# The layer normalisation's scaling pass one exponential earlier, and each reciprocal right behind its transposition

## The chip, the cores and the metric

One Trainium2 chip, of which one NeuronCore runs the whole program. The metric is the device time of one launch in microseconds (us). Engine names follow the profile: PE is the matrix engine (PEld its weight loads), DVE the vector engine, ACT the scalar engine, POOL the GpSimd engine, and SP the queue that issues the DMAs.

## The reference

For `x` of shape (8, 512, 1024) and a context of shape (8, 512, 256), float32:

```
xn   = layernorm(x)
q    = xn in 32 heads of 32 columns; k = v = context in 8 heads of 32 columns (4 query heads share one)
w    = softmax(q k^T / sqrt(32))          # 512 x 512 for each batch and query head
x    = x + (w v)                          # cross attention
yn   = layernorm(x)
gate = sigmoid(slope_n * (sum_s (select_n . (yn - mu_n) / |yn - mu_n|)^2 - center_n)),  n = 0..7
n*   = argmax_n gate;  s = max_n gate     # for each row
mod  = bias[n*] + degen[n*] (update[n*]^T (yn - debias[n*]))
out  = x + (1 - s) * yn + s * mod
```

## The kernel before

The attention runs over 64 **units** (8 batches times 8 key heads). A unit is one key head with its 4 query heads: 4 x 4 = 16 **quarters**, where quarter `n` is the 128 keys of block `n // 4` against the 512 queries of head `n % 4`. Each quarter goes through PE (`score_keys`, L596: four matmuls into one PSUM bank), then ACT (L870: the exponential from the bank into `probs`, in SBUF). Three banks take turns for everything that passes here: quarters, the turned tiles of `x`, the turned maxima, and the denominators. A table worked out in Python (`bank_of`, `bank_before`) says which use follows which in a bank, and PE waits for the use before it to be read out.

Each unit is walked in four steps `t` = 0..3, and each engine has its own instruction list, written out in the order of the code and never reordered. In step `t` of unit `u`:

- PE scores, for a unit ahead, the raw maxima (`score_rows`, L558), which DVE reduces (`largest`, L933, 2.29 us each). This is a ping-pong on a single buffer: L558 waits for the last L933, and L933 for L558.
- PE scores a few quarters (L596), multiplies the exponentials with the values (`gather`, L610), and scores the rest of the step's quarters. In an **even** unit the steps take quarters 0-3, 4-8, 9-11 and 12-15; quarters 12 and 13 come ahead of the gather in step 3, and 14 and 15 behind it.
- The denominators of a unit are the column sums of `probs`. POOL adds two key blocks at a time (`front`, L367, and `back`, L357, 4.56 us each), PE multiplies the two sums with ones (L623, L633), DVE transposes the result (`take_denominators`, L945) and takes 16 reciprocals for each partition (`invert`, L951), and POOL multiplies the turned rows with them (`normalise`, L329) and adds them to `x` (L334).

Units go in pairs. Below, E is an even unit and O = E + 1 the odd one behind it. In the pair, one new tile of `x` (128 rows) is prepared for a later batch: DVE takes its statistics (L961, L965, L971, L977), POOL the inverse root (L270, L273), ACT scales and shifts it (`normalise_tile`, L808, 1.23 us) in E, and in O PE turns it in three parts (L584), which ACT and DVE split into two halves of float16 (L819 and L985, L823 and L991). Tiles come to an end before the units do: E = 0, 2, ..., 50 have an L808 among their exponentials, E = 52 to 62 have none.

Behind the 64 units comes the gate stage over 8 batches (L707 to L741, L881, L1071 to L1145), which the change does not touch.

The places the change touches: `NORM_AT` (L198) is the quarter ahead of whose exponential `normalise_tile` stands in ACT's list; `invert` stands in DVE's list in the loop over `u` and `t` (L1047, L1059). Ahead of each exponential ACT waits for the quarter's scores. Ahead of quarters 0, 4, 8 and 12 it also waits for the gather and the POOL sum that last read that part of `probs`; these waits stand in the code ahead of `normalise_tile` for quarter 12.

Of the kernel before, what the change touches and what calls it, by code (L numbers as in the profile page):

```python
# [4 lines left out]
def xattn_ffn(nc: bass.Bass, x, ctx_in, sel_w, sel_mu, imp_center, imp_slope, lora_up, lora_dn,  # L5
# [34 lines left out]
    def wait(eng, sem, count):  # L40

        if not isinstance(count, int) or count > 0:
            eng.wait_ge(sem, count)

    with ExitStack() as keep:
# [55 lines left out]
        with ExitStack() as own:  # L101
# [86 lines left out]
            live = lambda u: 0 <= u < UNITS  # L188
# [6 lines left out]

            BEGIN = ((0, 4, 9, 12, NSC), (0, 5, 10, 13, NSC))
            MIDST = ((2, 6, 11, 14), (2, 7, 12, 15))
            NORM_AT = 13  # L198
            DOWN_AT, FOLD_AT = ((-AHEAD, ST - 1), (1 - AHEAD, 0)), (1 - AHEAD, ST - 1)

            QUARTERS_KEPT = {"score": 0.4, "max": 0.4, "part": 0.95}
# [581 lines left out]
            def _(act):  # L783
# [14 lines left out]
                def make_shift(u):  # L798

                    wait(act, max_turned, u + 1)  # L800
                    wait(act, shift_in[u % 2], 16 * (u // 2))
                    act.activation(shift[:, u % 2, :], st_ps[0:G * ST, bank_of["max", u, 0], 0:P], ACT.Copy,
                                   scale=-1.0 / SHIFT_UNIT).then_inc(shift_made, 1)

                def normalise_tile(n):

                    act.wait_ge(rstd_done, 2 * n + 2)
                    act.activation(x_tile(n), x_tile(n), ACT.Identity, scale=rstd[:, n % 2:n % 2 + 1],  # L808
                                   bias=neg_mean[:, n % 2:n % 2 + 1]).then_inc(xn_done, 1)
# [37 lines left out]
                for u in range(-AHEAD, UNITS):  # L847
                    tile = tile_of(u)
                    for t in range(ST):
# [8 lines left out]
                        if live(u):  # L858
                            s = u % 2
                            for n in range(BEGIN[u % 2][t], BEGIN[u % 2][t + 1]):  # L860
# [4 lines left out]
                                if n == MIDST[u % 2][2] and live(u + 1):  # L865
                                    make_shift(u + 1)
                                if n == NORM_AT and u % 2 == 0 and whole(tile):
                                    normalise_tile(tile)
# [50 lines left out]
            def _(dve):  # L919
                def first_largest(u, t):  # L920

                    for half in range(2):
                        wait(dve, max_scored if half else half_scored, ST * u + t + 1)
                        dve.reduce_max(row_max[:, u, 2 * half * ST + t:2 * (half + 1) * ST:ST],
                                       s_ps[:, 2 * half:2 * half + 2], AX.X
                                       ).then_inc(reduced if half else half_reduced, 1)

                def largest(u, t):

                    if t == 0:  # L930
                        wait(dve, max_turned, u - 1)
                    wait(dve, max_scored, ST * u + t + 1)
                    dve.reduce_max(row_max[:, u % 2, t:G * ST:ST], s_ps[:], AX.X).then_inc(reduced, 1)  # L933

                def take_rows(u):

                    wait(dve, pv_done, ST * (u + 1))
                    wait(dve, o_made, u - 1)
                    dve.transpose(o_t[:, u % 2, :], o_ps[:]).then_inc(o_taken, 1)  # L939

                def take_denominators(u):

                    wait(dve, den_done, u + 1)
                    wait(dve, inv_made, u)
                    dve.transpose(den_t[:], st_ps[:, bank_of["den", u, 0], :]).then_inc(den_taken, 1)  # L945

                def invert(u):

                    wait(dve, den_taken, u + 1)
                    wait(dve, o_made, u - 1)  # L950
                    dve.reciprocal(inv[:, u % 2, :], den_t[:, 0:S:D]).then_inc(inv_made, 1)  # L951
# [6 lines left out]
                def first_moments(n):  # L958

                    x_landed(dve, n)  # L960
                    dve.bn_stats(stats[:, n % 2, 0, :], x_tile(n)[:, 0:512])  # L961

                def last_moments(n):

                    dve.bn_stats(stats[:, n % 2, 1, :], x_tile(n)[:, 512:1024]).then_inc(stats_done, 1)  # L965

                def variance(n):

                    dve.wait_ge(stats_done, n + 1)
                    wait(dve, rstd_done, 2 * (n - 1))  # L970
                    dve.bn_aggr(mv[:, n % 2], stats[:, n % 2]).then_inc(mv_done, 1)  # L971

                def guard(n):

                    k = n % 2
                    dve.wait_ge(mv_done, n + 1)
                    dve.tensor_scalar_add(var_eps[:, k:k + 1], mv[:, k, 1:2], EPS).then_inc(var_ready, 1)  # L977

                def low_part(n, i):

                    cols = slice(n % 2 * P, (n % 2 + 1) * P)
                    dve.wait_ge(high_done, PIECES * n + i + 1)
                    bank = st_ps[:, bank_of["part", n, i], :]
                    if i == 0:
                        dve.scalar_tensor_tensor(out=k_parts_of(n)[:, 1, :, cols],  # L985
                                                 in0=bank[:, 0:CE].rearrange("p (c s) -> p c s", s=P), scalar=UP,
                                                 in1=k_parts_of(n)[:, 0, :, cols], op0=ALU.mult, op1=ALU.subtract
                                                 ).then_inc(low_done, 1)
                    else:
                        heads = slice(4 * i - 4, 4 * i)  # L990
                        dve.scalar_tensor_tensor(out=q_parts_of(n)[:, 1, heads, cols],  # L991
                                                 in0=bank.rearrange("p (c s) -> p c s", s=P), scalar=UP,
                                                 in1=q_parts_of(n)[:, 0, heads, cols], op0=ALU.mult, op1=ALU.subtract
                                                 ).then_inc(low_done, 1)

                def statistics(n):
                    moments(n)
                    variance(n)
                    guard(n)
# [21 lines left out]
                def sum_last(half):  # L1021

                    u, first = UNITS - 1, 2 * half
                    dve.wait_ge(exped, NSC * u + NSC // 2 * (half + 1))
                    dve.wait_ge(den_done, u - 1 + half)
                    dve.tensor_tensor(sums[:, (2 * u + half) % SUMS], probs[:, u % 2, first], probs[:, u % 2, first + 1],
                                      ALU.add).then_inc(last_sums, 1)

                for u in range(-AHEAD, UNITS + 1):
                    n = tile_of(u)  # L1030
                    early, late = live(u) and u % 2 == 0 and whole(n + 1), u % 2 == 1 and whole(n)
                    for t in range(ST):
                        if u == 1 - AHEAD and t == 2:
                            statistics(FIRST + 1)
                        if 0 <= maxima_at(u, t)[0] < HALVED:
                            first_largest(*maxima_at(u, t))
                        elif live(maxima_at(u, t)[0]):
                            largest(*maxima_at(u, t))
                        if late and t < PIECES:
                            low_part(n, t)  # L1040
                        if u == UNITS and t == 0:
                            sum_last(1)
                        if t == 0 and live(u - 1):
                            take_rows(u - 1)
                        if t == 1 and live(u - 2) and u % 2 == 0:
                            take_denominators(u - 2)
                        if t == (2 if u % 2 == 0 else 1) and live(u - 2):  # L1047
                            invert(u - 2)
                        if early and t == 0 and u == 0:
                            first_moments(n + 1)  # L1050
                        if early and t == 2:
                            last_moments(n + 1)
                        if late and live(u) and whole(n + 1) and t == 2:
                            variance(n + 1)
                        if late and live(u) and whole(n + 1) and t == ST - 1:
                            guard(n + 1)
                        if live(u) and u % 2 == 1 and t == ST - 1 and whole(tile_of(u + 1) + 1):
                            first_moments(tile_of(u + 1) + 1)
                        if t == ST - 1 and live(u - 1) and live(u) and u % 2 == 0:  # L1059
                            take_denominators(u - 1)  # L1060
                        if u * ST + t in range(ST * UNITS - 6, ST * UNITS - 2):
                            row_moments(0, 0, u * ST + t - (ST * UNITS - 6))
                        if u == UNITS - 1 and t == 2:
                            sum_last(0)
# [144 lines left out]
```

## Time and profile before

| | |
|---|---|
| median of 3 runs | 1076.25 us (1074.51, 1076.25, 1078.44) |
| the profiled execution's own time | 1074.34 us |
| its span in the trace | 1072.5 us |
| mean granted clock of PE in it | 0.986 |
| PE busy | 957.6 us (89%) |
| DVE busy | 914.0 us (85%) |
| POOL busy | 801.7 us (75%) |
| ACT busy | 738.8 us (69%) |
| chain that ended last, by engine | PE 61%, ACT 14%, DVE 13%, issue 6%, POOL 3% |
| chain that ended last, L808's share | 3% |

The span is what the trace covers; the execution's own time has 1.84 us around it. A timeline row gives the start in us from the span's start, the duration, the engine, the line and the operation, how many instructions were merged, and in brackets how long the engine stood idle before it and whose end it was waiting for. The "busy" of an engine says little by itself here: four engines are each above two thirds. What counts is which wait ends last at a place.

### The profile page before, as it was taken

What the parts mean: (1) busy time and instruction counts of PE and PEld (TensorE: products, weight loads), DVE (VectorE), ACT (ScalarE), POOL (GpSimd) and SP (SyncE); (2) the same over time, 40 slices, a digit from 0 to 9 for tenths busy, and PEclk for the clock granted to TensorE, in tenths of its full rate; (3) what the DMA queues carried; (4) which work ended last, traced back from release to release, by engine and by line L of the source; (5) the groups of instructions that cost most, each with busy time, mean ns of one, the idle gap of its engine ahead of it and who ended that gap; (6) DMA issues with size and microseconds to landing.
All of it is one profiled execution on the core that took longest, in us unless ns stands there. A gap on an engine that the chain in (4) does not pass through costs nothing.

```text
span 1072.5 us, 24586 instructions
## 1 busy us (share of the span) xinstructions
PE 957.6 (89%) x9518; PEld 374.4 (35%) x9518; DVE 914.0 (85%) x1106; ACT 738.8 (69%) x1301; POOL 801.7 (75%) x454
## 2 busy tenths in 40 slices
PE   4779999999999999999999999999999997999997
PEld 3222222222222222222222222222222224777773
DVE  6968888888888888888888888888888884898976
ACT  5457777777777777777777777777777776544540
POOL 7258888888888888888888888888999998312210
PEclk9889999999999999999999999999999998999999
DMA  7765676766676666666666666655665735656423
GB/s 249 196 141 126 136 160 141 157 144 143 152 155 150 147 153 144 155 141 157 147 155 145 155 146 156 146 131 121 140 137 118 182 77 156 188 207 220 171 119 156
DMA packets 319875, 164.18 MB, mean 153 GB/s; under 512 B 182216, under 2 KB 307240, under 8 KB 319760
## 3 DMA queue, kind: packets, MB, share of 16 engines
q1 hardware_dynamic: 319456, 161.76, 61.5%
q8 instruction: 76, 1.25, 0.5%
q0 software_dynamic: 304, 0.85, 0.4%
q14 instruction: 39, 0.32, 0.1%
HBM read 107.58 MB, written 54.53 MB: 151 GB/s over the span
## 4 chain that ended last, share of the span: by engine, by line
PE 61%; ACT 14%; DVE 13%; issue 6%; POOL 3%; SPq 2%; DMA 2%; DVEq 0%; ACTq 0%; POOLq 0%
PE psum L596 18%; PE psum L610 14%; ACT probs L870 10%; PE psum L558 6%; PE psum L633 6%; DVE row_max L933 5%; PE psum L623 5%; PE psum L741 4%; PE psum L719 3%; ACT xa L808 3%; PE psum L584 2%; DVE probs L1145 2%; DVE prod_mem L991 2%; PE psum L707 1%; POOL sums L357 1%
## 5 line engine op out<-in xcount | busy, mean ns | idle before, releaser
L870 ACT ACTIVATE probs<-psum 128x512 f32<-128x512 f32 x1024 | 565.4, 597 | 177.9 <-PE psum L596 153.3
L933 DVE TENSOR_REDUCE row_max<-psum 128x4 f32<-128x2048 f32 x248 | 568.1, 2291 | 99.9 <-PE psum L558 98.2
L596 PE MATMUL psum<-q_stack,k_stack 97*32 97x512 f16 x4096 | 357.2, 387 | 70.2 <-ACT probs L870 58.0
L367 POOL TENSOR_TENSOR sums<-probs 128x2048 f32<-128x2048 f32 x63 | 286.9, 4555 | 34.8 <-ACT probs L870 34.8
L357 POOL TENSOR_TENSOR sums<-probs 128x2048 f32<-128x2048 f32 x63 | 287.0, 4556 | 31.6 <-ACT probs L870 29.0
L610 PE MATMUL psum<-probs,v_in 128*32 128x512 f32 x2048 | 267.8, 597 | 0.0
L596 PEld LDWEIGHTS psum<-q_stack,k_stack 97*32 97x32 f16 x4096 | 96.5, 94 | 363.7 <-ACT probs L870 277.3
L558 PE MATMUL psum<-high_mem 32*128 32x512 f16 x992 | 98.0, 385 | 6.6 <-DVE row_max L933 6.6
L329 POOL TENSOR_TENSOR o_t<-o_t,inv 128x512 f32<-128x512 f32 x64 | 67.1, 1048 | 44.5 <-DVE inv L951 44.5
L334 POOL TENSOR_TENSOR o_all<-o_all,o_t 128x512 f32<-128x512 f32 x64 | 81.2, 1269 | 9.2
L610 PEld LDWEIGHTS psum<-probs,v_in 128*32 128x32 f32 x2048 | 64.0, 111 | 43.8 <-issue 2.1
L341 POOL TENSOR_SCALAR var_eps<-mv 128x1 f32<-128x1 f32 x32 | 9.3, 291 | 87.6 <-DVE mv L1019 87.0
L719 PE MATMUL psum<-w_all,high_mem 128*128 128x136 f32 x512 | 66.3, 283 | 6.0 <-DVE den_t L945 5.9
L633 PE MATMUL psum<-sums,ones 128*32 128x512 f32 x512 | 68.1, 604 | 0.0
L719 PEld LDWEIGHTS psum<-w_all,high_mem 128*128 128x128 f32 x512 | 63.7, 194 | 10.2 <-issue 9.7
L741 PE MATMUL psum<-down,probs 128*128 128x512 f32 x128 | 62.9, 620 | 4.3 <-DVE probs L1145 3.5
L623 PE MATMUL psum<-sums,ones 128*32 128x512 f32 x512 | 66.2, 592 | 0.0
L558 PEld LDWEIGHTS psum<-high_mem 32*128 32x128 f16 x992 | 25.0, 91 | 103.0 <-DVE row_max L933 66.2
L881 ACT ACTIVATE high_mem<-psum 128x1024 f32<-128x1024 f32 x32 | 32.4, 1014 | 38.5 <-PE psum L707 38.5
L939 DVE STREAM_TRANSPOSE o_t<-psum 128x512 f32<-128x512 f32 x64 | 45.6, 712 | 10.7 <-PE psum L610 5.4
L584 PE MATMUL psum<-ident,xa 128*128 128x128 f32 x256 | 46.1, 313 | 8.4 <-DVE probs L991 3.8
L823 ACT ACTIVATE prod_mem<-psum 128x512 f16<-128x512 f32 x60 | 35.8, 597 | 18.2 <-PE psum L584 18.2
(119 smaller groups left out, 759.3 us busy)
## 6 DMA issues: line engine op xcount, KB each, us to landing
q_stack<-q_split SPq DMA_DIRECT2D x192, 128.0 KB, 3.4
xa<-in_x_dram SPq DMA_DIRECT2D x32, 512.0 KB, 3.7
o_all<-in_x_dram SPq DMA_DIRECT2D x256, 64.0 KB, 2.4
x_attended<-o_all SPq DMA_DIRECT2D x64, 256.0 KB, 4.6
out_dram<-probs SPq DMA_DIRECT2D x32, 512.0 KB, 2.9
q_split<-prod_mem SPq DMA_DIRECT2D x15, 1024.0 KB, 5.5
xa<-x_attended SPq DMA_DIRECT2D x16, 512.0 KB, 4.5
probs<-x_attended SPq DMA_DIRECT2D x16, 512.0 KB, 4.6
```

The source lines that it names most:

```text
L334: pool.tensor_tensor(o_all[:, half, :, h, :], o_all[:, half, :, h, :], turned_rows, ALU.add).then_inc(o_made, 1)
L357: pool.tensor_tensor(sums[:, (2 * u - 1) % SUMS], probs[:, (u - 1) % 2, 2], probs[:, (u - 1) % 2, 3], ALU.add).then_inc(back_done, 1)
L367: pool.tensor_tensor(sums[:, 2 * u % SUMS], probs[:, u % 2, 0], probs[:, u % 2, 1], ALU.add).then_inc(front_done, 1)
L558: last = pe.matmul(s_ps[:, g, :], q_high[rows, u % SLOTS, t * P:(t + 1) * P], k_high[rows, u % SLOTS, :], start=True, stop=True)
L596: last = pe.matmul(st_ps[row:row + D, bank_of["score", u, n], :], k_stack[:, u % SLOTS, t * P + row:t * P + row + D], q_stack[:, u % SLOTS ...
L610: last = pe.matmul(o_ps[g * D:(g + 1) * D, :], v_in[:, u % 2, t, :], probs[:, u % 2, t, g, :], start=(t == 0), stop=(t == ST - 1))
L623: pe.matmul(st_ps[g * D:(g + 1) * D, bank_of["den", u, 0], :], ones[:, 0:D], sums[:, 2 * u % SUMS, g, :], start=True, stop=False)
L633: last = pe.matmul(st_ps[g * D:(g + 1) * D, bank_of["den", u, 0], :], ones[:, 0:D], sums[:, (2 * u + 1) % SUMS, g, :], start=False, stop=True)
L719: last = pe.matmul(z_ps[:, t % 2, 0:WC], yT[:, t % 2, c, :], w_all[:, c, :], start=(c == 0), stop=(c == EC - 1))
L741: last = pe.matmul(result_bank(n)[:, half * 512:(half + 1) * 512], mixT[:, t, :], down[:, half * 512:(half + 1) * 512], start=True, stop=True)
L870: act.activation(probs[:, s, keys, g, :], st_ps[:, bank_of["score", u, n], :], ACT.Exp, scale=EXP_SCALE).then_inc(exped, 1)
L933: dve.reduce_max(row_max[:, u % 2, t:G * ST:ST], s_ps[:], AX.X).then_inc(reduced, 1)
```

## The change

Two edits. First, `NORM_AT` goes from 13 to 12, so in even units ACT's scaling pass over the tile stands ahead of quarter 12's exponential and no longer ahead of quarter 13's. Second, DVE takes the reciprocals directly behind the transposition that they read: for an even unit in step 1 of the unit two later (before: step 2, behind another maximum), for an odd unit in step 3 of the unit behind it (before: step 1 of the unit after that).

```
-            NORM_AT = 13
+            NORM_AT = 12
...
                         if t == 1 and live(u - 2) and u % 2 == 0:
                             take_denominators(u - 2)
-                        if t == (2 if u % 2 == 0 else 1) and live(u - 2):
                             invert(u - 2)
...
                         if t == ST - 1 and live(u - 1) and live(u) and u % 2 == 0:
                             take_denominators(u - 1)
+                            invert(u - 1)
```

ACT's list in an even unit before, from quarter 8 on (L870 is an exponential, L802 the negated maxima of the next unit, L808 the scaling pass):

```order
L870 ACTIVATE probs<-psum 128x512 [waits scored,back_done,pv_done]
L870 ACTIVATE probs<-psum 128x512 [waits scored] x2
L802 ACTIVATE shift<-psum 16x128 [waits shift_in1,max_turned]
L870 ACTIVATE probs<-psum 128x512 [waits scored]
L870 ACTIVATE probs<-psum 128x512 [waits scored,back_done,pv_done]
L808 ACTIVATE xa<-xa,neg_mean,rstd 128x1024 [waits rstd_done]
```

The same place after the change:

```order
L870 ACTIVATE probs<-psum 128x512 [waits scored,back_done,pv_done]
L870 ACTIVATE probs<-psum 128x512 [waits scored] x2
L802 ACTIVATE shift<-psum 16x128 [waits shift_in1,max_turned]
L870 ACTIVATE probs<-psum 128x512 [waits scored]
L808 ACTIVATE xa<-xa,neg_mean,rstd 128x1024 [waits rstd_done,back_done,pv_done]
L870 ACTIVATE probs<-psum 128x512 [waits scored] x4
```

L808 has moved up by one exponential, and it has taken over quarter 12's two waits on `probs`, `back_done` (POOL's sum) and `pv_done` (the gather).

DVE's list before, from an odd unit's step 0 to the next even unit's step 2 (L939 and L945 are the transpositions of the attention's rows and of the denominators, L951 the reciprocals):

```order
L939 STREAM_TRANSPOSE o_t<-psum 128x512
L933 TENSOR_REDUCE row_max<-psum 128x4
L991 SCALAR_TENSOR_TENSOR prod_mem<-psum,prod_mem 128x4x128
L951 RECIPROCAL inv<-den_t 128x16
...
L939 STREAM_TRANSPOSE o_t<-psum 128x512
L933 TENSOR_REDUCE row_max<-psum 128x4
L945 STREAM_TRANSPOSE den_t<-psum 128x512
L933 TENSOR_REDUCE row_max<-psum 128x4
L951 RECIPROCAL inv<-den_t 128x16
```

And after the change, over the same stretch:

```order
L939 STREAM_TRANSPOSE o_t<-psum 128x512
L933 TENSOR_REDUCE row_max<-psum 128x4
L991 SCALAR_TENSOR_TENSOR prod_mem<-psum,prod_mem 128x4x128
L933 TENSOR_REDUCE row_max<-psum 128x4
...
L939 STREAM_TRANSPOSE o_t<-psum 128x512
L933 TENSOR_REDUCE row_max<-psum 128x4
L945 STREAM_TRANSPOSE den_t<-psum 128x512
L951 RECIPROCAL inv<-den_t 128x16
L933 TENSOR_REDUCE row_max<-psum 128x4
```

The odd unit's L951 is gone from its place behind the first L991 and now stands behind the L945 of the even unit's step 3, and the even one has moved up past one L933. PE's and POOL's lists are the same in both kernels.

## Rows read from the trace of the kernel before

**Rows 1.** Windows view: one pair with L808, one without. Columns by its first line.
```profile
core 0: us, PE busy (x) PEld busy (x) DVE busy (x) ACT busy (x) POOL busy (x), PEclk, DMA share, GB/s
496.71:523.76 27.05, 24.62 (x273) 7.78 (x269) 23.99 (x21) 20.64 (x39) 23.50 (x10) 1.00 0.56 123
778.71:803.00 24.29, 22.56 (x266) 6.73 (x258) 21.13 (x15) 17.82 (x34) 22.79 (x9) 1.00 0.64 137
```
**Rows 2.** Chain of waits, step 3 of an even unit: start, us, what.
```profile
520.82 0.60 ACT probs L870
521.41 1.13 ACT xa L808
```
**Rows 3.** Timeline of PE, the same step and the start of the odd unit.
```profile
520.29 0.62 PE L596 MATMUL psum<-q_stack,k_stack 97*32 97x512 f16 x8
...
521.59 0.40 PE L596 MATMUL psum<-q_stack,k_stack 97*32 97x512 f16 x4
523.08 0.40 PE L596 MATMUL psum<-q_stack,k_stack 97*32 97x512 f16 x4 [1.09 <-ACT probs L870]
523.41 0.39 PE L558 MATMUL psum<-high_mem 32*128 32x512 f16 x4
523.74 0.44 PE L584 MATMUL psum<-ident,cin 128*128 128x128 f32 x2
```
**Rows 4.** Timeline of ACT, the same stretch.
```profile
518.34 0.60 ACT L870 ACTIVATE probs<-psum 128x512 f32<-128x512 f32 x1
520.82 0.60 ACT L870 ACTIVATE probs<-psum 128x512 f32<-128x512 f32 x1 [1.87 <-PE psum L596]
521.31 1.23 ACT L808 ACTIVATE xa<-xa,neg_mean,rstd 128x1024 f32<-128x1024 f32 x1
522.44 1.69 ACT L870 ACTIVATE probs<-psum 128x512 f32<-128x512 f32 x3
524.21 0.38 ACT L819 ACTIVATE k_parts<-psum 128x256 f16<-128x256 f32 x1
```
**Rows 5.** Timeline of PE: unit 1's first scores, then the first and last such wait.
```profile
60.35 1.05 PE L596 MATMUL psum<-q_stack,k_stack 97*32 97x512 f16 x8 [4.19 <-DMA q_stack<-shift]
...
90.20 0.40 PE L596 MATMUL psum<-q_stack,k_stack 97*32 97x512 f16 x4 [1.09 <-ACT probs L870]
...
739.52 0.40 PE L596 MATMUL psum<-q_stack,k_stack 97*32 97x512 f16 x4 [1.09 <-ACT probs L870]
```
**Rows 6.** Timeline of DVE: both places at which a reciprocal arrives.
```profile
515.22 0.71 DVE L945 STREAM_TRANSPOSE den_t<-psum 128x512 f32<-128x512 f32 x1
516.47 2.29 DVE L933 TENSOR_REDUCE row_max<-psum 128x4 f32<-128x2048 f32 x1 [0.55 <-PE psum L558]
...
521.74 0.70 DVE L945 STREAM_TRANSPOSE den_t<-psum 128x512 f32<-128x512 f32 x1
523.86 2.29 DVE L933 TENSOR_REDUCE row_max<-psum 128x4 f32<-128x2048 f32 x1 [1.41 <-PE psum L558]
```
**Rows 7.** Timeline of DVE behind the last unit: a reciprocal right behind its transposition.
```profile
905.16 0.67 DVE L945 STREAM_TRANSPOSE den_t<-psum 128x512 f32<-128x512 f32 x1
905.87 0.25 DVE L951 RECIPROCAL inv<-den_t 128x16 f32<-128x16 f32 x1
906.04 0.64 DVE L1016 BATCH_NORM_STATS2 stats<-xa 128x6 f32<-128x512 f32 x1
```
**Rows 8.** Timeline of DVE, step 3 of an even unit without L808.
```profile
789.52 0.70 DVE L945 STREAM_TRANSPOSE den_t<-psum 128x512 f32<-128x512 f32 x1
790.51 2.29 DVE L933 TENSOR_REDUCE row_max<-psum 128x4 f32<-128x2048 f32 x1 [0.29 <-PE psum L558]
```
**Rows 9.** Timeline of POOL: a back sum and a normalise.
```profile
511.17 4.56 POOL L357 TENSOR_TENSOR sums<-probs 128x2048 f32<-128x2048 f32 x1
...
530.41 1.05 POOL L329 TENSOR_TENSOR o_t<-o_t,inv 128x512 f32<-128x512 f32 x1 [1.65 <-DVE inv L951]
```
**Rows 10.** Waits view, whole span: us in total, times, longest.
```profile
POOL o_t L329 <- DVE inv L951: 44.5, 31, 1.8
```

More of the change, by code:

```diff
@@ L197, in xattn_ffn @@
             MIDST = ((2, 6, 11, 14), (2, 7, 12, 15))
-            NORM_AT = 13
+            NORM_AT = 12
             DOWN_AT, FOLD_AT = ((-AHEAD, ST - 1), (1 - AHEAD, 0)), (1 - AHEAD, ST - 1)
@@ L1046, in _ @@
                             take_denominators(u - 2)
-                        if t == (2 if u % 2 == 0 else 1) and live(u - 2):
                             invert(u - 2)
@@ L1060, in _ @@
                             take_denominators(u - 1)
+                            invert(u - 1)
                         if u * ST + t in range(ST * UNITS - 6, ST * UNITS - 2):
```

## The prediction

> **What bounds the kernel now.** I read the page's chain of waits first: PE holds most of it, and one line of ACT that is no exponential, L808, stands in it too, which is odd for a pass that nobody needs soon. Second, the windows view, for the length of a pair of units: 27.05 us where the pair has an L808, 24.29 us where it has none, with PE at full granted clock (1.00) in both and no engine full in either: PE 24.62 busy of 27.05, DVE 23.99, POOL 23.50, ACT 20.64 [rows 1]. So the pair's length is set by handovers, and the question is which ones. Third, the timelines of PE and ACT in step 3 of an even unit. ACT stands idle for 1.87 us until quarter 12's scores are there, runs its exponential from 520.82, then L808 from 521.31, and only at 522.44 quarter 13's [rows 4]. PE has scored quarter 14 at 521.59 and wants to score 15, whose bank is that of quarter 13 (the bank table says so), so it stands until 523.08: 1.09 us idle, ended by ACT's L870 [rows 3]. The chain runs through exactly these pieces: exponential 12, then 1.13 us of L808 [rows 2]. The wait comes back in every pair with the same size: the first at 90.20, the last at 739.52, 649.3 us or 24 pairs of 27.05 apart, so 25 of them [rows 5].
>
> **Edit 1, L808 ahead of exponential 12.** The ACT queue is free from about 518.9 (exponential 11 starts at 518.34, and the next may start some 0.54 later), and exponential 12 cannot start before 520.82, since its scores are made by PE at 520.29 behind work that doesn't change [rows 3, 4]. L808 costs ACT 1.13 us from its start to the next one's (521.31 to 522.44). Put at 518.9 it is through at about 520.05, 0.75 us before exponential 12 is wanted. The cover is ACT's own wait for PE; if it were gone, each pair would lose up to 1.13 us in front of exponential 12 instead. The two waits that L808 takes over are long met: `back_done` is the POOL sum that ends at 511.17 + 4.56 = 515.73 [rows 9], and the gather of two units ago is older. What is queued behind L808 is exponential 12, and behind that PE's quarter 14.
>
> With L808 gone from between them, exponential 13 starts at 521.31 and ends at 521.91. Quarter 15's scores can follow 0.04 later, at 521.95; PE is itself ready at 521.59 + 0.33 = 521.92 (0.33 is the pace from 523.08 to 523.41), so 0.03 of the wait is left, and PE is 1.13 us ahead [rows 3]. ACT then: exponential 14 from 522.03 (scores at 521.59 + 0.40, and 0.04), exponential 15 at 522.58, and L819 at 522.58 + 0.54 = 523.12 against 524.21 before, so ACT is 1.09 ahead [rows 4]. From there both go into the odd unit, whose next PE wait is again one for ACT. I take the smaller, 1.09 us for each pair; the sizes differ by 0.04, and that is 1.0 us over all.
>
> What is late next? Three things come within 0.2 us of the new times. The turned part of the tile (L584, now at 523.74 - 1.13 = 522.61) uses the bank of the denominators, which are out at 521.74 + 0.70 = 522.44: 0.17 us to spare [rows 3, 6]. The odd unit's first quarters need exponentials 14 and 15 (522.63 and 523.18), and come at about 522.98 and 523.2. And DVE's L933, now at 523.86 - 1.13 = 522.73, has the moved reciprocal in front of it, next. A pair without L808 has the same step in that faster order, and its L933 waits only 0.29 us for PE [rows 8], so the order can run.
>
> Sum of edit 1: 25 pairs x 1.09 = 27.25 us. Unit 0 also has an L808, but unit 1's first scores wait 4.19 us for a DMA [rows 5], and what shifts by under 1 us in front of that is worth nothing.
>
> **Edit 2, the reciprocals.** 63 of the 64 are moved. What one costs behind its transposition is seen behind the last unit, where one stands so already: the transposition starts at 905.16, the reciprocal at 905.87, the next instruction at 906.04 [rows 7]. So the instruction behind may start 0.71 + 0.17 = 0.88 us after L945 does. Three places:
> - Even unit's step 1: 515.22 + 0.88 = 516.10, and L933 starts at 516.47, because PE's L558 makes it wait [rows 6]. Hidden by 0.37 us.
> - Even unit's step 3: 521.74 + 0.88 = 522.62 against L933's new start, 522.73. Hidden by 0.11 us. Without edit 1 there would be 1.2 us.
> - Pairs without L808: 789.52 + 0.88 = 790.40 against 790.51 [rows 8]. Hidden by 0.11 us.
>
> The Trainium skill, "VectorE: DVE Perf Modes", section "The DRAIN you can't avoid", speaks against this edit: it states that behind every DVE operation the pipe drains for about its duration less 266 ns before the next one starts, and that the semaphore costs nothing extra. Read so, a 0.70 us transposition would hold the reciprocal 0.43 us longer; L933 would come some 0.4 us late in the 6 late pairs, where PE waits for it, which makes the sum 2.4 us worse, about 1051. The trace disagrees: the gap is 0.04 us [rows 7].
>
> Where the reciprocals left, DVE was waiting for PE anyway, so nothing comes back there. What does go is POOL's wait: 44.5 us in 31 waits [rows 10], such as the 1.65 us at 530.41 [rows 9], since the odd unit's reciprocals are now there from about 522.7. POOL is not what anybody waits for: 23.50 busy in a pair of 27.05, and still below the new 25.96 [rows 1]. The bounds of edit 2: a gain is left out but for a fraction, because no engine waits for POOL anywhere inside a pair, so its 1.65 us would have to matter through nobody; a loss is at most 0.14 us a pair, 4.3 us over 31 pairs, if a chained reciprocal took twice its 0.25 us against a margin of 0.11. I cost it at nothing, by the one row that shows it chained [rows 7]. Neither edit issues or moves a DMA, and the lists of PE, POOL and SP stay as they are.
>
> **Sum.** The profiled execution took 1074.34 us (span 1072.5). 1074.34 - 27.25 = 1047.1 us. The median of the runs shown stands 1.9 us above it, and from there the same sum gives 1049.0. I forecast 1048.6 us. No step of this is in the gate stage, which keeps its length.
>
> **Rivals.**
> - *Partly given back on DVE or on a bank.* L808's time goes, but one of the three margins of 0.1 to 0.2 us fails, and the new wait eats 0.3 to 0.5 us of each pair: 1048.6 + 25 x 0.4 = 1059. For it: the margins are thin, and L558 and L933 are a ping-pong in which lateness is handed on. Against: in PE's list the next L558 stands behind the turned part, five quarters and a gather, so a small delay of L933 is swallowed.
> - *Nothing comes of it.* Exponential 13 isn't what quarter 15 waits for, or a POOL sum or a transfer of the negated maxima sets the pair at 27.05. Then 1076. Against: all 25 waits are of one size, end 0.04 us after the exponential, and a pair without L808 runs in 24.29; of the missing 2.76 us L808's 1.13 are one part, and PE's three turned parts (0.44 us for the first [rows 3], the others twice as large) the rest.
> - *Slower: L808 now delays quarter 12.* The place is exponential 12; the mechanism is that L808 starts late, because what it waits for (POOL's mean and root, POOL's back sum) isn't there. Each us past 519.69 (520.82 less 1.13) delays exponential 12 by as much, and from 1.09 us on the pair is longer than before. At 1.5 us it would be 25 x 0.4 = 10 us slower, 1086. Against: the back sum ends at 515.73, 4.0 us before that point, and the root is older still; L808 has never waited for POOL in a pair.
>
> **How the numbers follow.** Forecast 0.82; partly given back 0.12; nothing 0.03; slower 0.03. The range 1044 to 1056 us is the forecast with 1.0 us for the two sizes of the term, 2 us for where a median of few runs falls, a further gain of 1 to 2 us if POOL's relief counts somewhere, the 4.3 us of edit 2, and the nearer half of the first rival (25 x 0.3 = 7.5 us). It leaves out about 2 in 10. A difference of 0.3%, 3.2 us, is what a measurement of this kernel can tell from none: faster by more than that holds in the first two cases, 0.94; within it 0.03; slower 0.03.
>
> **What would show it.** In the profile after: a pair of 25.96 us between repeats of the same L329; L808 starting about 518.9 of the pair shown, with ACT's idle time ahead of exponential 12 down from 1.87 to some 0.7 us; no PE wait of 1.09 us before quarter 15; POOL's waits for `inv` almost gone; L808 no longer in the chain; late pairs still 24.29. The forecast is wrong if PE shows a new wait of over 0.2 us for DVE or ACT in the step behind, if L933 starts later than 0.5 us after its L558, or if exponential 12 starts later after quarter 12's scores than it does now.

## The result, and the profile after

The changed kernel takes 1043.78 us (median of 4 runs, 1043.33 to 1045.61) against 1075.85 us (4 runs). The ratio is 0.970 with a 95% interval of 0.968 to 0.972. The forecast was 1048.6 us with a range from 1044 to 1056: the sign and the mechanism hold, but the kernel gains 4.8 us more than I said and lies 0.2 us below my range. The profiled execution took 1044.04 us with a span of 1042.2 us, 30.3 us under that of before.

Where those 30.3 us are is read off one fixed mark, POOL's L329 in the even units. The 25 pairs with an L808 are 28.9 us shorter. The stretch behind the last pair, from the L329 of unit 60 to the next, was 16.38 us and is 15.43, 0.95 shorter. The first L329 comes 0.29 us earlier, and the rest is 0.15 us. First the windows view of the changed kernel, one pair with an L808 and one without, with the columns of [rows 1]:

```profile
482.00:507.90 25.90, 24.54 (x272) 7.75 (x272) 24.15 (x22) 20.64 (x40) 23.56 (x11) 1.00 0.61 124
...
759.22:783.50 24.28, 22.56 (x266) 6.72 (x258) 21.31 (x15) 17.83 (x34) 22.74 (x9) 1.00 0.56 122
```

A pair is 25.90 us, not the forecast 25.96, against 27.05 of before; one without L808 has kept its 24.3 [rows 1]. Now ACT in step 3 of an even unit, where [rows 4] had 1.87 us of idle time and L808 behind exponential 12:

```profile
499.54 0.60 ACT L870 ACTIVATE probs<-psum 128x512 f32<-128x512 f32 x1
500.03 1.23 ACT L808 ACTIVATE xa<-xa,neg_mean,rstd 128x1024 f32<-128x1024 f32 x1
501.93 1.09 ACT L870 ACTIVATE probs<-psum 128x512 f32<-128x512 f32 x2 [0.67 <-PE psum L596]
503.22 1.09 ACT L870 ACTIVATE probs<-psum 128x512 f32<-128x512 f32 x2 [0.21 <-PE psum L596]
504.24 0.38 ACT L819 ACTIVATE k_parts<-psum 128x256 f16<-128x256 f32 x1
```

L808 stands where ACT was idle, 0.67 us of the idle time are left, and ACT now waits for PE ahead of exponential 14. L819 starts 2.75 us behind the start of quarter 12's scores (504.24 - 501.49), where it stood at 3.92 (524.21 - 520.29). The same step on PE, and its next wait for ACT, in the odd unit:

```profile
501.49 0.62 PE L596 MATMUL psum<-q_stack,k_stack 97*32 97x512 f16 x8
...
502.78 0.69 PE L596 MATMUL psum<-q_stack,k_stack 97*32 97x512 f16 x8
503.40 0.39 PE L558 MATMUL psum<-high_mem 32*128 32x512 f16 x4
503.79 0.41 PE L584 MATMUL psum<-ident,cin 128*128 128x128 f32 x2
...
506.54 0.40 PE L596 MATMUL psum<-q_stack,k_stack 97*32 97x512 f16 x4 [0.34 <-ACT probs L870]
```

Quarters 14 and 15 now stand in one row, the wait of 1.09 us [rows 3] is gone. Count every row from quarter 12's scores (520.29 before, 501.49 now): L558 stood at 3.12 and stands at 1.91 us, 1.21 earlier; the turned part L584 stood at 3.45 and stands at 2.30, 1.15 earlier. Between those two rows 0.06 us are given back: L584 starts 0.39 us behind L558, not 0.33. DVE, with the moved reciprocal, shows why:

```profile
500.73 2.29 DVE L933 TENSOR_REDUCE row_max<-psum 128x4 f32<-128x2048 f32 x1 [0.17 <-PE psum L558]
502.94 0.71 DVE L945 STREAM_TRANSPOSE den_t<-psum 128x512 f32<-128x512 f32 x1
503.68 0.25 DVE L951 RECIPROCAL inv<-den_t 128x16 f32<-128x16 f32 x1
503.85 2.29 DVE L933 TENSOR_REDUCE row_max<-psum 128x4 f32<-128x2048 f32 x1
```

L945 reads the denominators until 503.65, and L584, which takes their bank, follows 0.14 us behind. The reciprocal starts 0.03 us behind the end of its transposition. An estimate from the Trainium skill's page "VectorE: DVE Perf Modes", "The DRAIN you can't avoid" (the duration less 266 ns), would put some 0.4 us between them, if the drain comes on top of the duration that the profile gives; read so, this trace disagrees again, with 0.03 us. L933 starts 0.06 us behind L558's end at 503.79, as it did before (523.86 against 523.80, [rows 3, 6]), so the reciprocal was covered. POOL no longer waits ahead of the odd unit's normalise (against 1.65 us in [rows 9]). The timeline, and then the waits view of the whole span (us in total, times, longest):

```profile
508.91 1.05 POOL L329 TENSOR_TENSOR o_t<-o_t,inv 128x512 f32<-128x512 f32 x1
```

```profile
POOL o_t L329 <- DVE inv L951: 1.8, 1, 1.8
```

Last, the place that I had costed at nothing: DVE and POOL around the end of unit 63's exponentials, after the change. L1026 adds two key blocks of `probs` in POOL's stead, and L341, L344 and L347 are POOL's one-column steps to a root.

```profile
863.91 2.25 DVE L1026 TENSOR_TENSOR sums<-probs 128x2048 f32<-128x2048 f32 x1
868.08 2.29 DVE L1026 TENSOR_TENSOR sums<-probs 128x2048 f32<-128x2048 f32 x1 [1.93 <-PE psum L633]
...
864.43 1.85 POOL L347 TENSOR_SCALAR neg_mr<-mv,rstd 128x1 f32<-128x1 f32 x1
...
867.35 0.27 POOL L347 TENSOR_SCALAR neg_mr<-mv,rstd 128x1 f32<-128x1 f32 x1
...
868.68 1.82 POOL L347 TENSOR_SCALAR neg_mr<-mv,rstd 128x1 f32<-128x1 f32 x1
...
871.79 1.05 POOL L329 TENSOR_TENSOR o_t<-o_t,inv 128x512 f32<-128x512 f32 x1
```

And the same in the kernel before:

```profile
892.06 0.25 DVE L951 RECIPROCAL inv<-den_t 128x16 f32<-128x16 f32 x1 [0.24 <-issue]
...
893.61 2.25 DVE L1026 TENSOR_TENSOR sums<-probs 128x2048 f32<-128x2048 f32 x1
897.30 2.29 DVE L1026 TENSOR_TENSOR sums<-probs 128x2048 f32<-128x2048 f32 x1 [1.44 <-PE psum L633]
...
893.65 2.34 POOL L347 TENSOR_SCALAR neg_mr<-mv,rstd 128x1 f32<-128x1 f32 x1
...
897.40 2.27 POOL L341 TENSOR_SCALAR var_eps<-mv 128x1 f32<-128x1 f32 x1
...
901.97 1.05 POOL L329 TENSOR_TENSOR o_t<-o_t,inv 128x512 f32<-128x512 f32 x1
```

A POOL step over one column takes 0.27 us, but one that begins while L1026 runs ends only 0.08 to 0.13 us behind L1026. Without the reciprocal at 892.06 in DVE's way, L1026 comes 5.13 us behind the start of POOL's last back sum, not 5.61, hits POOL later in its chain, and costs it 1.85 - 0.27 + 1.82 - 0.27 = 3.1 us. Before, it was 2.34 - 0.27 + 2.27 - 0.23 = 4.1. In both kernels the chain of waits stays on POOL from the back sum through all these steps to L329 and L334, and goes from there into the gate stage. The reciprocal took 0.48 us of DVE's list there, its own 0.25 and 0.24 of idle time ahead of it.

### The profile page after: what moved, and what is told of

Read it like the earlier page. It is cut to its first block, busy times and chain, and to the rows that moved or that the text cites. A ratio compares the mean times of both kernels' runs of the same rounds, so it can differ in the third digit from the quotient of the medians.

```text
span 1042.2 us, 24586 instructions
## 1 busy us (share of the span) xinstructions
PE 954.0 (92%) x9518; PEld 372.9 (36%) x9518; DVE 918.6 (88%) x1106; ACT 736.8 (71%) x1301; POOL 802.6 (77%) x454
## 4 chain that ended last, share of the span: by engine, by line
PE 65%; DVE 15%; ACT 8%; issue 7%; POOL 3%; DMA 0%; SPq 0%; DVEq 0%; POOLq 0%; ACTq 0%
PE psum L596 19%; PE psum L610 17%; ACT probs L870 8%; DVE row_max L933 6%; PE psum L558 6%; PE psum L633 5%; PE psum L623 5%; PE psum L741 4%; PE psum L719 4%; PE psum L584 3%; DVE probs L1145 2%; DVE prod_mem L991 2%; PE psum L707 1%; DVE row_max L924 1%; POOL sums L357 1%
## 5 line engine op out<-in xcount | busy, mean ns | idle before, releaser
L870 ACT ACTIVATE probs<-psum 128x512 f32<-128x512 f32 x1024 | 562.9, 596 | 150.4 <-PE psum L596 125.9
L933 DVE TENSOR_REDUCE row_max<-psum 128x4 f32<-128x2048 f32 x248 | 568.1, 2291 | 61.7 <-PE psum L558 61.3
L596 PE MATMUL psum<-q_stack,k_stack 97*32 97x512 f16 x4096 | 353.8, 387 | 44.5 <-ACT probs L870 31.0
L596 PEld LDWEIGHTS psum<-q_stack,k_stack 97*32 97x32 f16 x4096 | 97.0, 94 | 337.1 <-ACT probs L870 247.8
L558 PE MATMUL psum<-high_mem 32*128 32x512 f16 x992 | 97.8, 384 | 6.3 <-DVE row_max L933 6.3
L334 POOL TENSOR_TENSOR o_all<-o_all,o_t 128x512 f32<-128x512 f32 x64 | 81.5, 1274 | 9.2
L341 POOL TENSOR_SCALAR var_eps<-mv 128x1 f32<-128x1 f32 x32 | 7.3, 228 | 87.3 <-DVE mv L1019 86.7
L329 POOL TENSOR_TENSOR o_t<-o_t,inv 128x512 f32<-128x512 f32 x64 | 67.3, 1051 | 1.8 <-DVE inv L951 1.8
L558 PEld LDWEIGHTS psum<-high_mem 32*128 32x128 f16 x992 | 25.0, 91 | 102.4 <-DVE row_max L933 65.7
L584 PE MATMUL psum<-ident,xa 128*128 128x128 f32 x256 | 46.1, 313 | 9.5 <-DVE probs L991 3.8
L939 DVE STREAM_TRANSPOSE o_t<-psum 128x512 f32<-128x512 f32 x64 | 45.5, 712 | 9.4 <-PE psum L610 5.0
```

What stands on the lines that cost most here:

```text
L334: pool.tensor_tensor(o_all[:, half, :, h, :], o_all[:, half, :, h, :], turned_rows, ALU.add).then_inc(o_made, 1)
L558: last = pe.matmul(s_ps[:, g, :], q_high[rows, u % SLOTS, t * P:(t + 1) * P], k_high[rows, u % SLOTS, :], start=True, stop=True)
L596: last = pe.matmul(st_ps[row:row + D, bank_of["score", u, n], :], k_stack[:, u % SLOTS, t * P + row:t * P + row + D], q_stack[:, u % SLOTS ...
L870: act.activation(probs[:, s, keys, g, :], st_ps[:, bank_of["score", u, n], :], ACT.Exp, scale=EXP_SCALE).then_inc(exped, 1)
```

## Experiments

Two things were open: why a pair gains 1.155 us where ACT's side promised 1.09 and PE's 1.13, and what belongs to edit 2. Theory W: quarter 12's exponential carried three waits (scores, POOL's sum, the gather) and starts quicker with one; L808 has taken two of them over. Theory P: the stretch behind the last unit gains by edit 2, through the clash of L1026 with POOL. "Pair" is the distance of two L329 of even units. Where a kernel has lines more than the changed one, the line numbers behind them are higher (L873 or L876 is L870, L811 is L808).

**Edit 1 alone** (the kernel before with L198 changed):

```
-            NORM_AT = 13
+            NORM_AT = 12
```

> Edit 1 alone: the scaling pass ahead of quarter 12's exponential, the reciprocals where they were before. The pair of units measured 27.05 us before and 25.90 us after both edits, which is 1.15 us and not the forecast 1.09. Theory W (the extra 0.06 comes with edit 1: quarter 12's exponential no longer carries two more waits and starts 0.04 instead of 0.13 us after its scores): the pair is 25.84 to 25.90 us here too, POOL again waits about 1.6 us for each odd unit's reciprocals without anybody noticing, and the whole run is only the tail's 0.95 us longer than after, about 1045.0 us. Theory D (edit 2 gave it, by taking DVE's reciprocal out of the odd unit's step 1 or by freeing POOL): the pair is 25.96 us or longer, and the run 1046.5 us or more.

1047.89 us, ratio 0.975 (0.973 to 0.977). The pair is 25.90 us, as with both edits, so all of 1.155 us belongs to edit 1; the last stretch is 16.40 us, as before. The whole was forecast at 1045.0, and that missed: the profiled execution took 1046.22 us, its first L329 at 89.49 against 87.48 us in the changed kernel, and the median is 1.7 us above it. Medians of different groups of runs do not resolve 1 us here; the lengths of pairs do.

**Edit 2 alone** (the changed kernel with `NORM_AT = 13`):

> Edit 2 alone: the reciprocals behind their transpositions, the scaling pass still ahead of quarter 13's exponential. Theory W: the pair stays 27.05 us, POOL's waits for the reciprocals go, and only the stretch behind the last pair is shorter, by 0.95 us: about 1073.4 us in a profiled run, which a timed comparison cannot tell from before. Theory D: the pair is 26.99 us or shorter, 1.5 us or more less over 25 pairs, about 1071.8 us.

1074.39 us, 0.999 (0.998 to 1.001). The pair is 27.05 us, the last stretch 15.41. So edit 2 is worth 0.97 us at one place and nothing in any pair. A measurement of the whole cannot show that; the two marks in the trace can.

**The two waits back on exponential 12** (the changed kernel):

```
+    if n == NORM_AT and u % 2 == 0 and whole(tile):
+        normalise_tile(tile)
     if g == 0:
         ...            # the waits for the gather and for POOL's sum
...
-    if n == NORM_AT and u % 2 == 0 and whole(tile):
-        normalise_tile(tile)
```

> The kernel after, but with the two waits on probs (POOL's back sum and the older gather) put back on quarter 12's exponential, behind the scaling pass: nothing else moves. All waits are met long before. Theory W: the exponential of quarter 12 starts 0.13 us after its scores instead of 0.04, quarter 15's scores follow later by as much, and the pair grows from 25.90 by 0.06 to 0.09 us to 25.96 to 25.99, 1.5 to 2.2 us over 25 pairs. Theory D: where the waits hang is free, the pair stays 25.90 us.

1045.51 us, 0.973 (0.971 to 0.975); the pair is 25.925 us, +0.025. ACT and PE in the same step:

```profile
502.80 1.23 ACT L808 ACTIVATE xa<-xa,neg_mean,rstd 128x1024 f32<-128x1024 f32 x1
504.78 2.30 ACT L870 ACTIVATE probs<-psum 128x512 f32<-128x512 f32 x4 [0.75 <-PE psum L596]
```

```profile
504.26 0.62 PE L596 MATMUL psum<-q_stack,k_stack 97*32 97x512 f16 x8
...
506.25 0.39 PE L558 MATMUL psum<-high_mem 32*128 32x512 f16 x4
506.57 0.44 PE L584 MATMUL psum<-ident,cin 128*128 128x128 f32 x2
```

Quarter 12's scores end at 504.26 + 0.40 = 504.66, and the exponential starts 0.12 us later, as before the change (520.69 and 520.82, 0.13, [rows 3, 4]), not 0.04 later as in the changed kernel (501.89 and 501.93). L558 stands 1.99 us behind the scores, 1.13 earlier than before: L808 exactly. So the 0.08 us of W are real at that place. The chain of waits of the kernel before shows what fills them (L43 is the line of the helper that issues a wait):

```profile
520.71 0.02 issue
520.73 0.04 ACTq L43
520.77 0.04 issue
520.82 0.60 ACT probs L870
```

Between the scores and the exponential stands an instruction of ACT's queue that only waits, of 0.04 us, and 0.04 us behind it. It stands at the same place in this kernel, at 504.7, and ahead of exponential 0 of the changed kernel, at 518.1; ahead of exponential 12 of the changed kernel there is none. Ahead of an exponential with one wait the chain has 0.02 us of issue alone. Which of the three waits this instruction carries, the trace does not say.

The pair loses 0.025 of them and not the 0.06 to 0.09 that I expected, because L584 must wait for its bank in the changed kernel anyway: it stands at 2.31 us, against 2.30. The term is then 1.13 (L808) + 0.08 (the waits) - 0.06 (the bank).

**The same without the change** (the kernel before, quarter 12's two waits ahead of exponential 11):

```
-    if g == 0:
+    if g == 0 and not (n == 12 and u % 2 == 0):
         ...
+    if n == 11 and u % 2 == 0:
+        ...            # the same two waits
```

> The kernel before, but in even units the two waits on probs of quarter 12 stand one exponential earlier, on quarter 11's; in the 31 even units whose own step 3 sets the end, quarter 12's exponential then waits for its scores alone. Theory W: it starts 0.04 us after its scores instead of 0.13, and with it the scaling pass, exponential 13 and quarter 15's scores: the pair falls from 27.05 to about 26.97 us, 2.2 us over 25 pairs, about 1072.1 us in a profiled run. Theory D: 27.05 us, 1074.3.

1073.44 us, 0.998 (0.997 to 1.000). The pair is 26.975 us, 0.08 shorter, and those without L808 are 24.21 against 24.29. PE's wait ahead of quarter 15:

```profile
496.28 0.40 PE L596 MATMUL psum<-q_stack,k_stack 97*32 97x512 f16 x4 [1.01 <-ACT probs L873]
```

1.01 us for 1.09. Here nothing is near enough to swallow it, and W shows in full.

**W carried on** (the changed kernel; quarter 12's two waits ahead of 11, and quarter 0's ahead of the previous unit's quarter 15):

> The kernel after, with quarter 0's two waits on probs in even units moved one exponential earlier, onto quarter 15's of the odd unit before, and quarter 12's onto quarter 11's. Theory W (a third wait on an instruction for which its engine stands idle costs 0.09 us): quarter 0's exponential in even units follows its scores by 0.04 instead of 0.13 us, the five exponentials behind it move along, and the next wait of PE with them: 25.81 to 25.84 us for a pair and 24.20 for a late one, 31 pairs x 0.08 = 2.5 us faster than after, about 1041.6 us. Theory D, or a floor elsewhere that takes it (as the bank of the denominators took most of it for quarter 12): the pair stays at 25.90 us and the run where after is.

1047.06 us, 0.974 (0.972 to 0.976), for a forecast of 1041.6; the pair stays at 25.90, a miss. ACT and PE at an even unit's first quarters:

```profile
520.33 1.08 ACT L876 ACTIVATE probs<-psum 128x512 f32<-128x512 f32 x2 [1.71 <-PE psum L596]
521.62 2.27 ACT L876 ACTIVATE probs<-psum 128x512 f32<-128x512 f32 x4 [0.21 <-PE psum L596]
```

```profile
519.88 0.62 PE L596 MATMUL psum<-q_stack,k_stack 97*32 97x512 f16 x8
...
521.79 0.40 PE L558 MATMUL psum<-high_mem 32*128 32x512 f16 x4
522.27 0.89 PE L596 MATMUL psum<-q_stack,k_stack 97*32 97x512 f16 x8
```

Exponential 0 does start 0.05 us behind its scores, and L558 stands 1.91 us behind them, 0.09 earlier than in the changed kernel (519.66 - 517.66 = 2.00). The quarter behind L558 stands at 2.39 in both: it waits for exponential 2, which waits for its own scores and starts at 521.62. I had a real gain and no one who waits for it. Pairs without L808 are 24.20, by quarter 12's waits, 6 x 0.08 = 0.5 us, too little for the time to show.

**The cover** (the changed kernel; a second pass of ACT over the same tile, which leaves its values as they are, ahead of L808):

```
+    if n > FIRST + 1:
+        act.activation(x_tile(n), x_tile(n), ACT.Identity).then_inc(twice, 1)
+        act.wait_ge(twice, n - FIRST - 1)
```

> The kernel after, with the scaling pass of each tile of the 25 pairs preceded by an identity pass over the same tile (values unchanged), so ACT has twice the work in the same idle time. The idle time behind one pass is 0.67 us. If that is the cover, the second pass costs what sticks out of it: 1.23 + 0.04 + 1.13 = 2.40 us from the start of the first to exponential 12, against 1.90 us of free time, so quarter 12's exponential is 0.50 us late, and the pair, of which 0.06 us are waited for on the denominators' bank anyway, grows by 0.43 to 0.50 us: 26.33 to 26.40, about 11 to 12 us over all. Rival (ACT is the bound or the place itself matters): each pass costs its full 1.2 us, a pair of 27.1 us, 30 us in all. Other rival: the idle time isn't there, and nothing shows below 2 us.

1054.46 us, 0.981 (0.979 to 0.983); the pair is 26.155 us, +0.255, less than the 0.43 to 0.50 expected. ACT:

```profile
505.79 1.05 ACT L809 ACTIVATE xa<-xa 128x1024 f32<-128x1024 f32 x1
506.87 1.24 ACT L811 ACTIVATE xa<-xa,neg_mean,rstd 128x1024 f32<-128x1024 f32 x1
508.02 2.16 ACT L873 ACTIVATE probs<-psum 128x512 f32<-128x512 f32 x4
```

A pass without scale and bias columns takes 1.05 us, not 1.23, so the two passes hold ACT for 2.23 us and not for 2.40. Quarter 12's scores end at 507.65 and its exponential starts at 508.02, 0.37 behind instead of 0.04: 0.33 late, and the bank's 0.06 are swallowed again. 0.27 was to be seen, 0.255 is. Of the 1.10 us that the second pass adds to ACT's list (2.23 for 1.13), 0.33 come out late. So 0.77 us of ACT work beside L808 are free, and what goes beyond is paid, but for the bank's 0.06.

**L808 one place earlier, and two places later** (the changed kernel with `NORM_AT = 11`, then 14; 13 is edit 2 alone):

> The kernel after with the scaling pass one exponential earlier still, ahead of quarter 11's, so the two waits on probs are back on quarter 12's. The free time of ACT in step 3 of an even unit lies between exponential 11 and 12; a pass ahead of 11 only pushes 11 into it. Theory (only free time counts, not the exact place): exponential 11 ends 1.13 us later, which is 0.4 us before PE wants its bank for quarter 13, so nothing waits, and the pair is that of waits_on_12, 25.92 to 25.93 us, 0.6 us over 25 pairs. Rival (the bank of quarter 11 holds PE up, as quarter 13's did): a new wait before quarter 13, and a pair of 26.3 us or more.

1046.22 us, 0.973 (0.970 to 0.975), pair 25.925.

> The kernel after with the scaling pass on the other side, between exponentials 13 and 14. PE's wait of 1.09 us before quarter 15 was for exponential 13, so by that alone the wait would be gone here too. Theory (ACT is what everything behind waits for there, until its next idle time): exponentials 14 and 15 end 0.8 to 0.9 us later than after, the odd unit's quarter 1 (bank of quarter 15) and the gather of block 3 wait for them, L819 and the next five exponentials start 0.8 to 0.9 us later, and the pair is 26.65 to 26.8 us, some 20 us over all more than after. Rival (only the banks of quarters 12 and 13 matter): 25.9 us.

1067.81 us, 0.994 (0.991 to 0.996), pair 26.785. PE in the last:

```profile
520.80 0.79 PE L596 MATMUL psum<-q_stack,k_stack 97*32 97x512 f16 x8 [0.61 <-ACT probs L870]
```

One quarter earlier costs only what quarter 12's waits cost, since ACT's idle time takes L808 there too. Two quarters later, quarter 15 no longer waits, but PE waits 0.61 us in the next step, and 0.88 of the 1.155 us are gone; one quarter later, at 13, all of it is. The idle time ahead of exponential 12 is what pays, and both places in front of it reach it.

**The bank** (the changed kernel; the table lets the denominators' bank go later, and L584 takes quarter 14's):

```
-            DEN_TAKEN_AT = (ST + 2.0, 3.95)
+            DEN_TAKEN_AT = (ST + 2.0, 4.05)
```

> The kernel after with another bank for the first turned part of the tile: the table's time at which an odd unit's denominators leave their bank is set from 3.95 to 4.05, which hands that part the bank of quarter 14 and the odd unit's quarter 0 the bank of the denominators; the rest of the pair keeps its pattern. Theory B (L584 starts 0.39 us behind L558 instead of 0.33 because the denominators' transposition ends 0.14 us before it): now it waits for exponential 14, which ends at 503.82 against 503.65 for the transposition, so it starts 0.46 us behind L558 and the pair is 25.96 to 25.98 us. Rival (the 0.06 us aren't the bank's): 25.90 us.

1047.64 us, 0.975 (0.973 to 0.977); the pair is 26.06 us, +0.16, twice what I expected. ACT and PE:

```profile
504.91 1.08 ACT L870 ACTIVATE probs<-psum 128x512 f32<-128x512 f32 x2 [0.21 <-PE psum L596]
```

```profile
503.18 0.62 PE L596 MATMUL psum<-q_stack,k_stack 97*32 97x512 f16 x8
...
505.09 0.39 PE L558 MATMUL psum<-high_mem 32*128 32x512 f16 x4
505.65 0.41 PE L584 MATMUL psum<-ident,cin 128*128 128x128 f32 x2 [0.17 <-ACT probs L870]
```

L584 stands 2.47 us behind quarter 12's scores, 0.17 later than with the denominators' bank, and the pair pays 0.16 of it. Exponential 14 ends at 504.91 + 0.60 = 505.51, and L584 follows 0.14 us behind. I had reckoned with the 0.04 us by which L596 follows an exponential. The same 0.14 lies between L945's end and L584 in the changed kernel. So L584 follows a release 0.1 us later than L596 does; why, no run here tells.

**Unit 61's reciprocals in their old place** (the changed kernel; 61 is the last odd unit whose reciprocals edit 2 moves):

```
+                        if t == 1 and u == UNITS - 1:
+                            invert(u - 2)
...
-                            invert(u - 1)
+                            if u != UNITS - 2:
+                                invert(u - 1)
```

> The kernel after, but unit 61's reciprocals alone are back in their old place, step 1 of unit 63, amid the statistics of the gate stage's first tiles. Theory P (the 0.95 us that the stretch behind the last pair gained, 16.38 to 15.43 us between two normalises of POOL, come from DVE's first sum over probs starting 0.47 us earlier against POOL's small operations, which stand still beside that sum): 16.4 us again, POOL's two long operations in it 2.3 us each instead of 1.85, and the run 0.95 us longer than after. Rival: the stretch is shorter for another reason (POOL's normalise of unit 61, which no longer waits), and it stays at 15.4 us.

1045.42 us, 0.973 (0.972 to 0.975). The pair is 25.90, and the last stretch 16.38 us. DVE and POOL:

```profile
861.80 0.26 DVE L951 RECIPROCAL inv<-den_t 128x16 f32<-128x16 f32 x1 [0.22 <-issue]
...
863.36 2.25 DVE L1026 TENSOR_TENSOR sums<-probs 128x2048 f32<-128x2048 f32 x1
```

```profile
863.44 2.29 POOL L347 TENSOR_SCALAR neg_mr<-mv,rstd 128x1 f32<-128x1 f32 x1
...
867.15 2.29 POOL L341 TENSOR_SCALAR var_eps<-mv 128x1 f32<-128x1 f32 x1
```

One reciprocal of 0.26 us brings back all of the 0.95, and the clash looks as before. Theory P stands, and edit 2's whole effect is that one instruction.

**The changed kernel once more**, to see what a repeat of the same program does:

> The kernel after once more, unchanged, on the chip and in the rounds of the three others of this call: the pair 25.90 us, the run 1043.3 to 1046 us. Beside it the scatter of one kernel between executions is seen; the stretch up to POOL's first normalise has varied between 87.5 and 89.8 us from kernel to kernel so far, with nothing changed in it.

1045.35 us (1043.23 to 1050.22, 5 runs), 0.973 (0.971 to 0.976). Pair 25.90, last stretch 15.42. But from unit 60's L329 to the end of the span it takes 188.4 us, where the first execution took 185.8: the same program, 2.6 us apart. Its mean granted clock is 0.982 against 0.993; in six windows of 31 us from that L329 on, it is 0.89 against 0.94 in the first and again in the sixth, and 1.00 in the four between them in both. That the clock makes the 2.6 us was not tested.

None of these kernels was faster than the changed one by more than the measurement can tell.

## Why the prediction fell short

- *L808's time comes out of each pair, since exponential 13 holds quarter 15.* Right: alone it is exactly 1.13 us of PE's time (the two waits back on 12), and the cover of 0.75 us is there (the second pass).
- *The size of the term, 1.09 for each of 25 pairs.* Too small, and this is the step with the largest part: 1.155 was measured, 1.6 us in all. From two sizes I took the smaller one, read at ACT's L819, as if ACT set L819's time. It does not: L819 follows the end of PE's L584 by 0.03 us before (524.18, 524.21) and by 0.04 after (504.20, 504.24), and it came 1.17 us earlier and not 1.09. In the changed kernel the chain of waits runs on PE alone from 499.92 to 505.87 us, past all of step 3, so PE's 1.13 was the size that the pair has. That is 1.0 us. The rest is the two waits. I wrote that L808 takes them over and that they are long met, and priced them at nothing; even met, they cost their carrier 0.08 us. After the bank 0.025 of it is left.
- *Three margins of 0.17, 0.02 and 0.11 us hold* (exponential 15 at 523.18 for a quarter at 523.2 is 0.02; what I called 0.1 to 0.2 us for all three was wrong). The second and third did. The first was eaten up: with PE 1.21 us ahead it was 0.09 and not 0.17, and L584 follows its bank 0.14 us behind and not at once, so it waits some 0.06 us. It is the first rival in small, at the place named, and it is inside 1.155.
- *Edit 2 costs and brings nothing.* True in every pair, wrong behind the last one: 0.95 us. My reason for leaving a gain out was that nobody waits for POOL inside a pair. In the last stretch somebody does, and there the gain came by DVE's list being shorter by one instruction, not by POOL's wait for `inv`. I took the pair for the whole program. And "no step of this is in the gate stage" had the boundary wrong: this stretch stands between the pairs and that stage.
- *The anchor.* From the profiled execution the sum gave 1047.1; I moved it to 1048.6 toward the median of three runs. Over 35 later runs in three groups the kernel before had medians of 1074.5 to 1075.3 us, so those three lay 1 to 2 us high. That is 1.5 us of the 4.8. Between groups the changed kernel's own median goes from 1043.78 to 1045.35 us, so whether it falls below 1044 is luck; the 1.155 and the 0.95 us are read off the trace and come back in the repeat (25.90 and 15.42).
- *What else fills the 2.76 us between the two kinds of pair.* I took PE's second and third turned part for twice the 0.44 us of the first, which with L808's 1.13 is more than 2.76. They take 0.66 each in the trace. Nothing in the sum hung on it.

With the measured sizes, 1074.34 - 25 x 1.155 - 0.95 - 0.3 (start) = 1044.2 us, against the profiled 1044.04. The start's 0.3 us is within the scatter: the first L329 came between 87.8 and 89.3 us in the three executions with `NORM_AT = 13`, and between 86.4 and 89.8 in the ten others.

## What to carry to other kernels

A pass that someone needs late belongs into the idle time ahead of the instruction that waits longest. Here one place too early was nearly as good, one place too late gained nothing, and two too late gained a quarter. When the two engines of a handover give two sizes for one saving, ask of each place which engine set its time before, and count the bare waits that a moved instruction takes over or leaves behind. Look at the pairs and at the stretch behind the last one separately: there a change with no effect in any pair can hit a path of its own.

## What the hardware showed that I had not expected

- A wait that is long met is not free. With three waits, ACT's exponential starts 0.12 to 0.13 us behind its scores, with one 0.04 to 0.05 (two places, six kernels). The difference is an instruction of 0.04 us in ACT's queue and 0.04 us behind it.
- POOL stands still behind DVE's L1026, which reads two operands from SBUF: an operation over one column goes from 0.27 to 1.85 or 2.34 us. During L933, which reads PSUM, POOL's sums keep their 4.56 us. The Trainium skill has this rule, "SBUF — State Buffer", "Who interferes with whom": a DVE instruction with two SBUF inputs contends with a POOL instruction that reads SBUF. The trace agrees, and shows that the smallest operation can pay for the whole length of the other. Moving one reciprocal of 0.26 us changed that price by 0.95 us.
- PE's L584 (float32) follows the release of its bank by 0.14 us, L596 (float16) by 0.04.
- ACT's pass over 128x1024 takes 1.05 us without scale and bias columns and 1.23 with them.
